# Four graph layers on one core: the node stage ahead of the typed attention as one pipeline, value rows beside the score loop, broadcast rows in the message pass

## What is computed

```python
# layer 1: relational attention, per edge type r of 5
e = leaky(Qn[tgt] @ a_q + Kn[src] @ a_k)
attn = softmax of e over the edges of one target and type
h_prime += segment_sum(where(edge_type == r, Vn[src] * attn, 0), tgt)
x = x + elu(h_prime)
# layer 2: typed attention; Q, K, V by one of three matrices per node type, 8 heads of 16
kt = K[src] @ W_edge[edge_type]
scores = (Q[dst] * kt).sum(-1) / sqrt(16) * mu[:, edge_type].T
x = x + block(segment_softmax(scores) * V[src])     # with output product, norms, feed-forward
# layer 3: message passing
h = relu([x[src], x[dst], edge_attr] @ W1.T + b1)
agg = segment_sum(h @ W2.T + b2, dst)
```

## Time and profile before

| | |
|---|---|
| median of 3 runs | 5188.58 us (5188.26 to 5203.77) |
| the profiled execution: its own time | 5186.52 us |
| its span | 5184.8 us |
| mean granted clock of TensorE | 0.747 of 2.4 GHz |
| PE busy | 3185.8 us (61%) |
| POOL busy | 2938.1 us (57%) |
| DVE busy | 2685.6 us (52%) |
| ACT busy | 782.1 us (15%) |

### The profile page before, as it was taken

One profiled execution on the slowest core, in us unless ns is written; L12 is line 12 of the kernel. 1 busy time (PEld: TensorE's weight loads), 2 busy tenths in 40 slices (PEclk: granted clock), 3 DMA queues, 4 the chain that ended last, 5 costly groups with the idle time before them and its releaser, 6 DMA issues. The chain is left out here.

```text
span 5184.8 us, 84388 instructions
## 1 busy us (share of the span) xinstructions
PE 3185.8 (61%) x20680; PEld 2748.7 (53%) x20681; DVE 2685.6 (52%) x7818; ACT 782.1 (15%) x1810; POOL 2938.1 (57%) x2911
## 2 busy tenths in 40 slices
PE   0000298885777677775554676657776886566665
PEld 0000188885666566664552465445655884356663
DVE  5100288875444444445679655356664664344443
ACT  1000022222111111112100243100000001222222
POOL 3767677774777477771677740067773000077772
PEclk9999989886555555556655798855555997799997
DMA  6333355553222322222872573466654441022222
GB/s 214 75 87 77 93 153 151 150 140 76 76 76 77 60 77 75 76 76 62 214 202 88 172 193 100 109 170 174 175 171 106 123 127 47 4 72 62 62 61 32
DMA packets 631530, 561.85 MB, mean 108 GB/s; under 512 B 236605, under 2 KB 523650, under 8 KB 631426
## 3 DMA queue, kind: packets, MB, share of 16 engines
q0 software_dynamic: 99328, 211.51, 17.4%
q1 hardware_dynamic: 392322, 233.28, 15.5%
q10 hardware_dynamic: 139776, 115.91, 7.9%
HBM read 408.99 MB, written 151.40 MB: 108 GB/s over the span
## 5 line engine op out<-in xcount | busy, mean ns | idle before, releaser
L696 POOL DMA_INDIRECT ring<-table_gine,idx x1248 | 1244.2, 997 | 496.8 <-issue 370.3
L696 POOL DMA_INDIRECT ring<-table_msg,idx x416 | 425.0, 1022 | 725.4 <-SPq L191 598.9
L739 DVE TENSOR_TENSOR mraw<-ps,ring 128x512 f32<-128x512 f32 x416 | 287.4, 691 | 827.0 <-DMA ring<-table_gine,idx 372.4
L723 POOL DMA_INDIRECT arena<-table_keys_values,idx x416 | 429.7, 1033 | 466.1 <-SPq L191 337.8
L1777 PE MATMUL ps<-oh,msg 128*128 128x128 f32 x1664 | 425.5, 436 | 307.5 <-DVE HA L739 211.7
L714 POOL DMA_INDIRECT HA<-table_rel,idx x416 | 444.5, 1068 | 253.8 <-DMA table_rel<-arena 127.3
L739 DVE TENSOR_TENSOR HA<-HA,ps 128x128 f32 (+1 forms) x1664 | 476.5, 286 | 166.9 <-DVE HA L739 146.2
L1777 PEld LDWEIGHTS ps<-oh,msg 128*128 128x128 f32 x1664 | 366.4, 324 | 366.1 <-DVE HA L739 337.1
L1744 PE MATMUL ps<-wt,ear 65*128 65x128 f32 x2496 | 521.1, 379 | 16.7 <-DMA ear<-edge_attr_T 16.7
L682 POOL DMA_INDIRECT slot_records<-arena,slotr x400 | 390.3, 976 | 214.6 <-issue 122.2
L1744 PEld LDWEIGHTS ps<-wt,ear 65*128 65x128 f32 x2496 | 494.1, 293 | 17.4 <-issue 16.9
(11 more groups left out here) (332 smaller groups left out, 6062.1 us busy)
## 6 DMA issues: line engine op xcount, KB each, us to landing
ear<-edge_attr_T SPq DMA_DIRECT2D x312, 128.0 KB
ear<-slot_rows ACTq DMA_DIRECT2D x312, 128.0 KB
oh<-slot_rows ACTq DMA_DIRECT2D x104, 256.0 KB
slot_values<-HA SPq DMA_DIRECT2D x104, 256.0 KB, 2.8
ring<-slot_values ACTq DMA_DIRECT2D x104, 256.0 KB
slot_values<-arena SPq DMA_DIRECT2D x104, 256.0 KB, 3.8
ring<-slot_values SPq DMA_DIRECT2D x104, 256.0 KB, 3.0
slot_records<-msg SPq DMA_DIRECT2D x32, 650.0 KB, 11.7
```

Of the source, the lines that this page charges most:

```text
L696: pool.indirect_dma_start(out=ring[:, k % 4, j, 0:width], out_offset=None, in_=table[:, :], in_offset=bass.IndirectOffsetOnAxis(ap=idx[:, ...
L723: pool.indirect_dma_start(out=kvring[:, k % 4, j, :], out_offset=None, in_=tab2[:, :], in_offset=bass.IndirectOffsetOnAxis(ap=idx5[:, k * ...
L739: return V.tensor_tensor(o, x, y, op)
```

## The change

Three stages change. The value products move from ahead of the score loop into its first 25 turns (28 turns are unrolled for it, `HEADK` = 7). The node stage becomes a pipeline over 7 groups of four blocks: ELU and norm by groups, H turned once (25 transposes), masks made from the turned rows straight out of PSUM, with a row of node types that SP loads early, `mu` put into the weights instead of the keys. In the message pass ScalarE loads broadcast rows of target numbers, VectorE makes the turned one-hot from them in bf16, and the target's row is looked up in three bf16 parts. The opening and closing products become bf16.

```diff
@@ SP @@
+            sp.wait_ge(dve_made, mr_set)
+            load(types, a["node_type_3"].rearrange("(a n) -> a n", a=1).to_broadcast([P, N]))
-            join.to("tr_keysT")
-            for b in range(NBLK): ... V rows; join.to("tr_qv"); for b in range(NBLK): ... key rows
+            for z in range(GRP + 1):
+                if z < GRP:
+                    for b in group_blocks(z):
+                        sp.wait_ge(pn_free, free["qv", b // 2])
+                        sp.dma_start(t2b[b][:, :, 1, :], T3[4][:, b, :].unsqueeze(1).to_broadcast([P, NREL, D])).then_inc(t_out, 16)
+                if z:
+                    for b in group_blocks(z - 1):
+                        sp.wait_ge(cent, made["e4", z - 1])
+                        sp.dma_start(t2b[b][:, :, 0, :], kwb[:, (z - 1) % 2, b % 4, :]...)
@@ DVE, node stage @@
-            ch(V.tensor_scalar(neg, relsum, 0.0, None, ALU.min))
-            ...
-            norm(X[:, :, :], H[:, :, :], relu=True)
+            for z in range(GRP):
+                V.scalar_tensor_tensor(Xf[:, at], ps[:, z, 0:n], 0.0, Xf[:, at], ALU.max, ALU.add).then_inc(cent, 1)
+            for z in range(GRP + 1):
+                if z < GRP:
+                    V.scalar_tensor_tensor(Xf[:, at], T[0][:, at], -1.0, Xf[:, at], ALU.add, ALU.add).then_inc(cent, 1)
+                if z:
+                    for b in group_blocks(z - 1):
+                        V.bn_stats(lnst[:, b, :], X[:, b, :]).then_inc(bn_done, 1)
+            ... statistics, H = max(X - mean, 0) for 25 blocks, scaling of 7 of them (ScalarE has 18)
+            for i in range(GRP + 2):
+                if i < GRP:
+                    for t in range(NTYPE):
+                        V.scalar_tensor_tensor(MXT[:, i % 2, t, 0:n], TROW[:, at], float(t), ps[:, i % 2, 0:n], ALU.is_equal, ALU.mult).then_inc(cent, 1)
+                z = i - 2
+                if z >= 0:
+                    split([v[:, b0:b0 + nz, :] for v in QB], Qn[:, b0:b0 + nz, :], q_rest[:, 0:nz, :])
+                    V.tensor_copy(kwb[:, z % 2, 0:nz, 4 * D:], ps[:, 7, 0:nz * D]...)
@@ PE, node stage @@
-            turn_all(T3[3]); turn_all(T3[4]); turn_all(XL)
-            product(*[(WKb[:, t, :], T[t]) for t in range(NTYPE)])
-            ...
+            for i in range(GRP + 2):
+                if i < GRP: ... four transposes of H
+                z = i - 1
+                if 0 <= z < GRP: ... K product of group z, then Q and V of its blocks
+                z = i - 2
+                if z >= 0: ... K by edge type for the blocks of group z
@@ PE, value rows and score loop @@
-            for b in range(NBLK): ... L1866, L1867
+            def value_products(t):
+                ...
+            run(pe, [(2, lookups), (0, value_products)], head=HEADK)
@@ ACT @@
-            run(act, [(0, lookup_rows_in), (3, q_copied)])
+            run(act, [(0, lookup_rows_in), (1, value_rows), (3, q_copied)], head=HEADK)
@@ opening and closing of sums @@
-                M.matmul(ps[:, z, 0:n], b2row[0:1, :], any_row[:, 0:n], start=True, stop=False)
+                M.matmul(ps[:, z, :], zero_b, any_b, start=True, stop=False)
@@ message pass @@
+                split([v[:, b0:b0 + n, :] for v in NP], T3[2][:, b0:b0 + n, :], n_rest[:, 0:n, :])
+                V.tensor_scalar(oN[:, t.h], nrow[:, t.h], iota_p, None, ALU.is_equal).then_inc(qp["onehotT"], 1)
-            run(dve, [(4, acc_pair(qp, agg3, D + 1)), (2, mp_add), (0, onehots(qp["onehot"], qp["sums"], oh))])
+            run(dve, [(5, acc_pair(qp, agg3, D + 1)), (3, mp_add), (1, mp_dst_onehots), (1, onehots(qp["onehot"], qp["sums"], oh))])
-            run(act, [(2, relu(qp)), (0, onehotT(qp, lambda t: t.n))])
+            run(act, [(0, mp_rows_in), (4, relu(qp))])
-                    ins = M.matmul(o, ohT[:, t.h, j, :], rows_at(T3[2], D)(blocks[j]), start=False, stop=True)
+                    for i in range(3):
+                        ins = M.matmul(o, oN[:, t.h, j * P:(j + 1) * P], rows_at(NP[i], D)(blocks[j]), start=False, stop=(i == 2))
-            run(pe, [(3, sums(qp, D + 1, pair(D + 1))), (1, nd_mp), (0, turn_onehot(qp, own))])
+            run(pe, [(4, sums(qp, D + 1, pair(D + 1))), (2, nd_mp)])
```

320 lines of the change are left out of this document (197 added, 123 removed).

## The result

The changed kernel takes **5056.4 us** (median of four runs, 5048.58 to 5094.68) against 5194.78 for the kernel before on the same chip (four runs, 5188.26 to 5203.77). The medians differ by 138 us. The ratio, taken from the means with a fifth execution of 5055.12 us among them, is **0.9744, 95% interval 0.9698 to 0.9789**: faster. The prediction had 5086 us, in a range of 5050 to 5124. The profiled execution is the slowest of the four: 5094.68 with a span of 5093.0. The other three span 5046.8 to 5055.1.

What follows compares the result with a forecast made beforehand. POOL was taken to bound the message pass, with the node stage and the value-row-to-attention chain also on the path; −31 − 24 − 53 + 2 + 4 = −102 us from 5186.5 gave 5084.5, median 5086 us, range 5050 to 5124.

Steps and rivals of the forecast that it cites:

- the forecast's own row: Whole kernel: all parts come near their price, giving 5062 to 5112 us; chance 0.58.
- more than forecast: Rival: mixed turns of 2.2 us and node stage at its lower bound, 5063, with small gains elsewhere 5050; chance 0.14.
- Value rows beside the score loop: Score loop: value products move into its turns, about 27 mixed turns of 2.6 us; −31 us, between −43 and 0.
- My bound from below: Mixed turns of the score loop: DMA of slot rows and table writes sets at least 2.2 us a turn.
- Opening and closing products: Attention loop's end and typed attention's second loop: bf16 products save 8, 9 and 7 us; −24, bounds −16 and −28.
- The node stage: Ahead of the `table_keys_values` gathers: 174.7 us becomes 122, −53; node-type broadcast during the attention loop adds +2.
- The bound of −64: Node stage: the gain if the keys by type cost 27 us and the clock nothing.
- The message pass: Message pass: POOL's 5.30 us period leaves nothing to gain, compares beside gathers cost; +4 us, bounds 0 and +63.
- the rival of the blocked POOL: Message pass: each added compare stops POOL for its whole length, 41 us, giving 5123 us; chance 0.04.

Runs made afterwards that it cites:

- again2: The changed kernel unedited, run on the third chip as the measure for kernels beside it: 5062.30 us, ratio 0.9775 to the kernel before; its profile spans 5054.6 us.
- phase: Changed kernel with the message pass's f32 one-hot comparison ahead of the bf16 comparison and accumulations on VectorE, no work added: 6177.89 us on the second, slow chip.

## Why the prediction was right, and where it wasn't

The range held, and faster was right. The median of 5056 lies below the 5062 to 5112 of the forecast's own row, beside the rival "more than forecast" (5063, down to 5050). Of that rival's two conditions one came: the node stage took 112.7 us, where it had 111. The other, mixed turns of 2.2 us, did not (2.95). What brought the time there was the message pass, which neither had. With the message pass as I forecast it, +4 in place of −28, it would have been 5088: the other parts came out right in their sum. That the whole still lay in the range is in part luck.

By its parts, against the profiles of the changed kernel:

- **Value rows beside the score loop, −31.** Measured −24.6 to −27.0 in the profiles, and 28 us when undone alone. Right in mechanism, and mis-sized in the mixed turn, 2.95 us against 2.6. I took the sum of TensorE at the upper clock, and the clock was up (0.95), but TensorE was busy for 75% of the time only. My bound from below counted a write as 0.82 us of DMA share; what sets the turn is that a write's landing keeps one of two buffers for 5.2 us. The gathers start at 2517 (forecast 2506), and 102 us of slack were left.
- **Opening and closing products, −24.** Measured 8.4 us (10.10 to 1.68), 9 to 11 and 7 to 8: 24 to 27. Right.
- **The node stage, −53 and +2.** Measured −62: 23.7 + 81.8 + 7.2 = 112.7 against my 25 + 84 + 5 + 8 = 122. The bound of −64 should read −62 (174.7 less 122 − 4 − 5 = 113). The sums from rows were each 1 to 2 us high, and the 5 us for a TensorE that starts at the lower clock were not needed on top: it did so (six K passes in 5.49 us, six later ones in 2.74), and the 81.8 us hold that loss. No gaps inside the pipeline, as assumed.
- **The message pass, +4.** Measured −27 to −29, and 27 us the other way when undone: this is the step that failed. The sentence was "The period is POOL's 5.30, so a gain has nothing to act on." The period is POOL's indeed, (4989.5 − 4467.3) / 415 × 4 = 5.03 us now, but I took the mean gather of 1022 ns for a constant of POOL, and the 11 ns between the means of two loops for the price of a compare. It held 0.94 us of gather and, on average, 0.08 us of a hold by VectorE's own f32 comparison, which the kernel's edit moved away without meaning to; the same comparison put ahead in VectorE's order brought most or half of it back (1012 and 986 ns). The median of 944 and the mean of 1022 to 1068 in the earlier trace rows stood side by side; I used the median against the rival of the blocked POOL and did not ask what filled the gap. That TensorE's clock would come out between was right (0.83), with its wait of 9.6 us too small to matter; the splits are hidden.
- **The rival of the blocked POOL** was right as a mechanism and wrong in sign here: POOL is blocked, but the added compare took blocking away. The Trainium skill states it in two ways. Advanced Engine Details and Errata (VectorE Performance Modes) has the two-port modes and GpSimd blocking each other. No row names the mode of the bf16 comparison; it held a gather that started in it by 0.03 us on average in the message pass, and by up to 0.2 us in the typed loop. SBUF — State Buffer (SBUF: two separate sides) has an exclusive lock that operations with two SBUF inputs take as well, against a GpSimd operation that reads SBUF; the gather reads its row numbers from the SBUF tile `idx`. The trace agrees with the lock and shows this second kind as the costly one in the message pass: 0.32 us for each gather that starts inside. It also agrees that the one that starts first delays the other. It differs on how long: by the page the holder keeps the lock for its whole instruction, but a gather of 0.94 us lengthened a comparison by 0.08 us at most, and only one that started within 50 ns of it.
- **The second loop of the typed attention** I took as unchanged. It is, but it varies by 30 us between executions, and together with a tail that varies by 12 it is why a single profile of this kernel says −92 where the runs say −138.

With the sizes found: −26 − 26 − 62 − 28 = −142, and 4 to 5 us lost ahead of the first value product and 4 to 9 in the attention loop, where the unedited kernel's profiles have 284.5 to 289.9 us against 281.0: about −131. The profile of again2 has −130.2, the medians −138. Between −102 and −131 lie the message pass (32), the node stage (11) and the opening and closing products (2), less the value rows (5) and those small losses (about 11); why they were lost I did not test.

## What to carry to other kernels

Where a mean stands well above its own median, take the difference as a cost with a cause, and look at what the other engines do at the starts of the long ones. GpSimd's gathers were held here at their start by a VectorE comparison with two SBUF inputs, and by what stood behind it without a gap. In a loop whose turns are started by landed gathers, the cost depends on the offset between the two, so that an edit meant for something else can switch it: between none and 36 holds were counted in 200 us of one stage. Four short comparisons with a single tensor as their input removed it in one stage and halved it in another, where they stand back to back with other operations. Price a write into a table behind two buffers by its time from issue to landing, not by its share of the queues. Before reading a small gain from one profile, cut it into stages and see which stages differ between two profiles of the same kernel.

## What the runs showed of the hardware

- A gather that starts while VectorE runs an f32 comparison of 128x512 with two SBUF inputs lasts until 0.13 us before that operation's end, plus 0.94: 11.7 us measured against 12.1 by that rule over 36 starts (before), 8.2 against 8.5 over 26 (phase). With an operand in PSUM there is no hold (45 starts, 0.1 us). If a bf16 comparison follows without a gap, the gather goes on 0.12 us before the end of that one (typed loop, holds up to 0.94 us).
- A gather that starts in the comparison's first 25 to 40 ns, or just ahead of it, isn't held; the comparison takes up to 0.76 us in place of 0.68 (before) or 0.73 (the changed kernel).
- The same comparison as four f32 operations of 128x128 with a pointer scalar held 25 gathers for 0.25 us in all in the first network's layers; in the typed loop, back to back with a scan and a bf16 comparison, gathers were still held up to 0.81 us.
- TensorE, hardly pausing, stayed at 1.2 GHz for 12 to 104 us before its clock came up, for the same code, and cost up to 35 us. Ten added products a turn in the loop ahead didn't change that.
- A write of 320 KB from SBUF to a table landed 2.2 us behind its issue alone, and 5.2 us beside the score loop with its broadcast loads (medians of 25).
- One of the chips ran every kernel 1000 us slower. In its score loop the signal of TensorE's finished lookups came 41 us late while GpSimd gathered, with GpSimd's own gathers as short as elsewhere and ScalarE's loads landing within 5 us.
